# Dense experts of a gated four-layer block: the first product from half-precision parts that the pool engine makes of the weights

## The chip, the cores and the metric

One core of one Trainium2 chip runs the whole block as one program. The metric is the device time of one execution in microseconds (us), the slowest core's, and there is only one core here. Lower is better.

## The reference, cut to what matters

The block has four layers, each a gated cross-attention and a gated feed-forward part, on x of 16 batches x 112 rows x 256 columns. The change touches only the feed-forward part of layer 2: eight dense experts, expert e working on the two batches 2e and 2e+1 (224 rows).

```python
x = x + tanh(g_ffn[2]) * _L2_ffn_ref(_layernorm(x), w1, b1, w2, b2)

def _L2_ffn_ref(x, w1, b1, w2, b2):    # w1: 8 x 256 x 1024, w2: 8 x 1024 x 256
    tokens = x.reshape(E, T, D)        # E = 8 experts, T = 224 rows, D = 256
    h = jnp.einsum('etd,edf->etf', tokens, w1) + b1[:, None, :]
    h = jax.nn.gelu(h)
    y = jnp.einsum('etf,efd->etd', h, w2) + b2[:, None, :]
    return y.reshape(B, S, D)
```

## The kernel before

The program is a row of stages, each a block in which every engine has its own list of instructions; engines meet only through semaphores. A stage ends when its slowest engine ends. The dense experts are `experts_dense` (L1863), the sixth stage. Before it stands the attention of layer 2, behind it the one-head attention of layer 3 and its fp4 feed-forward part, whose weights are rounded ahead of time inside `experts_dense`.

**The body of one expert.** Every engine runs `body(turn)` through `skewed` (L1375), with `turn.i` the expert number. `there(i + 1, E)` says that a part for the next expert exists. A few turns are written out, the rest run in a loop of two turns. The order within each engine is fixed by the code.

- PE (L1997 on), in body(i): the four transposes of expert i+1's normed rows into PSUM bank 0 (L2005), which wait for the rows (`s_xn`); the second product of expert i (L2021), 2 row halves x 8 chunks with the gelu output as weights and w2 moving, which waits for the load of w2 and for all eight gelu chunks of the expert; then the first product of expert i+1 (L2031), 8 chunks f x 2 halves c of the contraction, all in float32, w1 as weights and the turned rows (224 columns) moving, into three PSUM banks in turn, each chunk waiting for the gelu of three chunks before. For the last expert eight matmuls of the next stage's weights (L2012) stand ahead of its second product.
- ACT (L1911 on), in body(i): copies expert i+1's turned rows from PSUM to `xnT` (L1921), then makes the eight gelu chunks `hT` (L1929).
- DVE (L1935 on), in body(i): norms the two batches of expert i+2 (L341, called at L1964) as soon as the transposes of i+1 have read the old ones; `gate_up_weights(i)` (called at L1968): eight steps of fp4 rounding (L2384 to L2422) on an eighth of the raw gate and up weights, 512 columns; then for each of the two batches the bias row (L1979), the residual with expert i's second product (L1983) and the statistics of the row (`row_stats`, L262 to L266, with a one-element memset of `carry`, L92, before some); then `down_weights(i)`: the same eight steps on 176 columns. The first `gate_up_weights` waits for the load of the raw fp4 weights (`s_wn`). Expert 6 adds a reciprocal root of 13 small steps (`row_rstd`), expert 7 the first rows of the next stage.
- SP issues all loads. At the start of the stage: the biases and the three raw fp4 weights (L2047, L2049, 704 KB each). In body(i): w1 of expert i+2 (1024 KB, L1856) once all first products of expert i are done (`s_h`), then w2 of expert i+1 (L1859) once the second product of expert i-1 is done (`s_y`). w1 of experts 0 and 1 and w2 of expert 0 are loaded during the attention before. All these loads go through one hardware queue.
- POOL has no block in this stage. In other stages it makes the half-precision parts of float32 tiles: a cast to float16 (L723, L784, L803) and the difference of the tile and its cast (L725, L786, L805); and it builds masks (L822), for 16 or 32 partitions, four instructions in a row.

**Where a product is already made of half-precision parts** (top-2 experts L1773, attention L1190 and L1282), each float32 operand is held as a high part (cast to float16) and a low part (rest), and three float16 matmuls stand for one in float32: high x high, high x low, low x high.

The two buffers of w1 are halves of one float32 tile (`g.fw[0]`), those of w2 halves of another (`g.fw[1]`). The lines that matter most:

```python
pe.wait_ge(s_gelu, (i + 1) * FT)                        # before the second product
held(sp, g, s_h, (i + 1) * FT)                          # before the load of w1 of expert i + 2
normed(dve, g, g.by_batch, (i + 2) * 2 + r, r).then_inc(s_xn, 1)
gate_up_weights(i)
```

## Time and profile before

| what | us |
|---|---|
| median of 3 runs | 1403.06 (1402.62 to 1405.44) |
| the profiled execution, its own time | 1411.71 |
| span of its profile, first to last instruction | 1409.9 |
| dense experts, first instruction of the block to the start of the next stage | about 1062.3 to 1179.7 |
| PE busy | 1312.7 (93% of the span) |
| DVE busy | 1105.6 (78%) |
| ACT busy | 694.4 (49%) |
| POOL busy | 414.9 (29%) |
| mean granted TensorE clock | 0.969 of 2.4 GHz |

Times in the profile count from the span's start. A float32 matmul shows as two records on PE and on PEld (the weight load), so the 16 float32 matmuls of one expert's first product are 32 records. PE's durations overlap, since matmuls are pipelined: what a series costs is read from its first start to the next thing's start. In the rows, "[1.29 <-X]" behind an instruction is the time that its engine stood idle before it, and X what ended that wait.

### The profile page before, as it was taken

What the parts mean: (1) busy time and instruction counts of PE and PEld (TensorE: products, weight loads), DVE (VectorE), ACT (ScalarE), POOL (GpSimd) and SP (SyncE); (2) the same over time, 40 slices, a digit from 0 to 9 for tenths busy, and PEclk for the clock granted to TensorE, in tenths of its full rate; (3) what the DMA queues carried; (4) which work ended last, traced back from release to release, by engine and by line L of the source; (5) the groups of instructions that cost most, each with busy time, mean ns of one, the idle gap of its engine ahead of it and who ended that gap; (6) DMA issues with size and microseconds to landing.
All of it is one profiled execution on the core that took longest, in us unless ns stands there. A gap on an engine that the chain in (4) does not pass through costs nothing. (4 is left out here: it accounts for less than half of the span.)

```text
span 1409.9 us, 36465 instructions
## 1 busy us (share of the span) xinstructions
PE 1312.7 (93%) x11864; PEld 977.7 (69%) x11864; DVE 1105.6 (78%) x3711; ACT 694.4 (49%) x1639; POOL 414.9 (29%) x580
## 2 busy tenths in 40 slices
PE   5999999899899999999899889999988998998998
PEld 3777878645457777776545568878877887885666
DVE  7788778678779988889678777676764885668997
ACT  2666767544345555555434356766753323442321
POOL 1333346434433444447134423432420000000000
PEclk8999999989989999999899999999999998999999
DMA  5544455231233333334011233333346351550000
GB/s 159 157 122 125 125 151 156 83 113 49 83 100 98 85 85 95 91 85 136 14 55 49 77 106 107 87 94 103 87 131 195 133 171 43 148 144 22 16 15 23
DMA packets 134073, 138.11 MB, mean 98 GB/s; under 512 B 38601, under 2 KB 121292, under 8 KB 133836
## 3 DMA queue, kind: packets, MB, share of 16 engines
q1 hardware_dynamic: 133948, 136.51, 33.6%
q8 instruction: 70, 1.15, 0.4%
q14 instruction: 55, 0.45, 0.1%
HBM read 100.98 MB, written 35.48 MB: 97 GB/s over the span
## 5 line engine op out<-in xcount | busy, mean ns | idle before, releaser
L1143 DVE TENSOR_REDUCE negm<-ps 112x1 f32<-112x375 f32 x512 | 260.7, 542 | 105.1 <-PE ps L1267 102.6
L1267 PE MATMUL ps<-kst,qst 96*112 96x375 f16 x768 | 232.5, 337 | 14.4 <-DVE negm L1143 7.1
L853 ACT ACTIVATE p<-ps 125x448 f32<-125x448 f32 x336 | 177.3, 543 | 110.2 <-PE ps L1295 71.9
L1282 PE MATMUL ps<-qst,kst 112*125 112x224 f16 (+1 forms) x1152 | 210.4, 265 | 8.0 <-POOL qst L822 4.3
L822 POOL TENSOR_TENSOR qst<-m_row,diag 16x448 f16<-16x448 f16 x128 | 130.3, 1046 | 280.1 <-ACT m_row L932 275.1
L1282 PEld LDWEIGHTS ps<-qst,kst 112*125 112x125 f16 (+1 forms) x1152 | 147.0, 138 | 43.1 <-issue 9.7
L1773 PE MATMUL ps<-fw,xs_e 128*128 128x512 f16 x672 | 162.7, 386 | 0.0
L1127 DVE TENSOR_SCALAR ps<-ps 125x448 f32<-125x448 f32 x192 | 120.0, 629 | 31.2 <-PE ps L1282 31.1
L1139 DVE CUSTOM_DVE_ANT_0 with_mask<-ps,mask_add 112x375 f16<-112x375 f32 x256 | 134.3, 545 | 11.5 <-issue 10.1
L1267 PEld LDWEIGHTS ps<-kst,qst 96*112 96x112 f16 x768 | 96.9, 131 | 47.5 <-DVE negm L1143 21.2
L1190 PE MATMUL ps<-wkv_split,ctxT 128*125 128x256 f16 x864 | 121.0, 277 | 0.4 <-DVE ks L1098 0.4
L1190 PE MATMUL ps<-ctxT,wkv_split 128*128 128x375 f16 (+1 forms) x552 | 107.5, 333 | 9.3 <-DVE ctxT L963 8.7
L1773 PEld LDWEIGHTS ps<-fw,xs_e 128*128 128x128 f16 x672 | 66.8, 99 | 66.7 <-issue 4.9
L822 POOL TENSOR_TENSOR mst<-m_row,mask_diag 32x448 f16<-32x448 f16 x64 | 64.1, 1031 | 158.2 <-ACT m_row L932 139.3
L1190 PEld LDWEIGHTS ps<-wkv_split,ctxT 128*125 128x125 f16 (+1 forms) x864 | 98.5, 138 | 3.0 <-issue 1.9
L853 ACT ACTIVATE p_a<-ps 125x448 f32<-125x448 f32 x144 | 78.2, 544 | 29.1 <-PE ps L1295 19.0
L1306 PE MATMUL ps<-p,v 125*32 125x112 f32 x2688 | 89.3, 266 | 0.0
L1295 PE MATMUL ps<-mst,mask_add 128*125 128x448 f16 x192 | 72.2, 385 | 12.0 <-DVE ps L1127 10.0
L1190 PEld LDWEIGHTS ps<-ctxT,wkv_split 128*128 128x128 f16 x552 | 54.3, 100 | 41.2 <-issue 14.7
L1306 PEld LDWEIGHTS ps<-p,v 125*32 125x32 f32 x2688 | 61.8, 111 | 20.1 <-issue 13.0
L2606 PE MATMUL ps<-wgu,xqT 128*128 128x512 f32 (+3 forms) x224 | 72.4, 478 | 3.4 <-DVE xh L2534 2.0
L1544 ACT ACTIVATE p<-ps,weight_e 128x256 f32<-128x256 f32 x112 | 47.0, 464 | 56.0 <-DVE weight_e L1753 52.0
(262 smaller groups left out, 2512.3 us busy)
## 6 DMA issues: line engine op xcount, KB each, us to landing
k_split<-ks SPq DMA_DIRECT2D x48, 375.0 KB, 3.6
kst<-k_split SPq DMA_DIRECT2D x96, 187.5 KB, 2.9
fw<-in_w SPq DMA_DIRECT2D x16, 1024.0 KB, 7.2
qst<-q_split SPq DMA_DIRECT2D x96, 112.0 KB, 2.4
kst<-k_split SPq DMA_DIRECT2D x96, 93.8 KB, 2.6
stage<-in_ctxT SPq DMA_DIRECT2D x16, 375.0 KB, 4.0
ctxn<-in_ctx SPq DMA_DIRECT2D x16, 375.0 KB
rows<-x SPq DMA_DIRECT2D x48, 112.9 KB, 2.8
```

The source lines that it names most:

```text
L822: pool.tensor_tensor(m_stack[q][m_rows, 4 * hg:4 * hg + 4, :], g.m_row[q][m_rows, :].rearrange("p (o s) -> p o s", o=1) .to_broadcast([n_m ...
L853: act.activation(p[p_of[hg]][kt], ps[0:KR, BK_ST + n % 2, 0:4 * S], ACT.Exp).then_inc(s_exp, 1)
L1127: dve.tensor_scalar(st, st, -CLIP, CLIP, ALU.max, ALU.min).then_inc(s_clip, 1)
L1139: dve.tensor_tensor_reduce(g.with_mask[h % 2][:, :], scored, g.mask_add[1 - par][0:S, :], 1.0, -3e38, ALU.add, ALU.max, g.maxima[1 - par][ ...
L1143: dve.tensor_reduce(g.negm[1 - par][:, h:h + 1], scored, AX_X, ALU.max, negate=True).then_inc(s_max, 1)
L1190: mm = pe.matmul(out, lhs(l, c), rhs(r, c), start=(k == 0), stop=(k == 3 * KC - 1))
L1267: mm = pe.matmul(ps[0:S, BK_S + h % 2, 0:SK], g.q_stack[q][0:96, h, :], g.k_stack[q][0:96, h // 2, :], start=True, stop=True)
L1282: mm = pe.matmul(bank[:, 2 * r * S:2 * (r + 1) * S], g.k_stack[par][0:rows, pr, kt * KR:(kt + 1) * KR], g.q_stack[par][0:rows, 2 * pr:2 * ...
L1295: pe.matmul(bank, g.mask_add[par][:, kt * KR:(kt + 1) * KR], g.m_stack[par][:, 4 * hg:4 * hg + 4, :], start=False, stop=True, skip_group_c ...
L1306: mm = pe.matmul(pv[32 * j:32 * j + 32, hg * S:(hg + 1) * S], g.v[par][:, kt, 4 * hg + j, :], p[p_of[hg]][kt][:, j * S:(j + 1) * S], start ...
L1773: mm = pe.matmul(out, lhs(l, c), rhs(r, c), start=(k == 0), stop=(k == 3 * KC - 1))
L2606: mm = pe.matmul(gate_up[w][:, first:last], xqT[:, c, :], wgu[:, w, c, first:last], start=(c == 0), stop=(c == KC - 1))
```

## The change

Expert 0 stays as it was, with its own tile `xnT0`. For experts 1 to 7 the first product becomes three float16 matmuls per chunk and half (48 of 224 columns instead of 16 in float32). POOL makes the parts of w1 in a new block (two casts of 128 x 1024 and two differences of the same size per expert, with a one-element `carry` before each cast), two experts deep. ACT's copy of the turned rows now writes their high part, and DVE makes the low part, behind the norming of the next rows and ahead of `gate_up_weights`. The load of w1 for expert i+2 no longer waits for the first product of expert i but for POOL's last difference of that expert. The second product's wait for all eight gelu chunks becomes one wait per chunk, in its first row half.

```diff
@@ -1870,6 +1870,7 @@
     s_w1, s_w2 = g.s_w1, g.s_w2
     s_xn, s_t, s_xnT, s_h, s_gelu, s_y, s_x = (sem(n) for n in ("xn", "transposed", "xnT", "h", "gelu", "y", "x"))
     s_rows, s_dve, s_m = sem("rows_counted"), sem("dve"), sem("wq_wk")
+    s_xhi, s_xlo, s_w1hi, s_w1lo, s_pool = (sem(n) for n in ("xnT_high", "xnT_low", "w1_high", "w1_low", "pool"))
     gate = g.gates[0:S, 6:7]
     FT = F // 128
     W = 2 * S
@@ -1880,7 +1881,10 @@
             return local.enter_context(nc.sbuf_tensor(f"{name}_d", shape, dt))
         b1 = sb("b1", [128, E, FT])
         b2 = sb("b2", [S, E, D])
-        xnT = [sb(f"xnT{i}", [128, KC, W]) for i in range(2)]
+        xnT0 = sb("xnT0", [128, KC, W])
+        xs = [sb(f"xs{i}", [128, 2, KC, W], F16) for i in range(2)]
+        w1s = [sb(f"w1s{i}", [128, 2, KC, F], F16) for i in range(2)]
+        turned = ps[:, 0, 0:KC * W].rearrange("p (c s) -> p c s", c=KC)
         hT = [sb(f"hT{i}", [128, FT, W]) for i in range(2)]
         acc = [sb(f"acc{i}", [S, D]) for i in range(2)]
         w1 = [g.fw[0][:, p * 2048:(p + 1) * 2048].rearrange("p (c f) -> p c f", c=KC) for p in range(2)]
@@ -1898,7 +1902,10 @@
                     i = turn.i
                     if there(i + 2, E):
 
-                        held(sp, g, s_h, (i + 1) * FT)
+                        if isinstance(i, int) and i == 0:
+                            held(sp, g, s_h, FT)
+                        else:
+                            held(sp, g, s_w1lo, i * KC)
                         load_dense(sp, a, g, Turn(turn.t + 1, turn.u), 0, s_w1)
                     if there(i + 1, E):
 
@@ -1908,6 +1915,25 @@
                         load_one_head_weights(sp, a, g)
 
                 skewed(Steps(sp, s_b), 0, 0, E - 1, 2, body)
+
+            @block.gpsimd
+            def _(pool):
+                def body(turn):
+                    i = turn.i
+                    q = 1 - turn.u
+                    if there(i + 1, E):
+                        pool.wait_ge(s_w1[q], 16 * (turn.half(1) + 1))
+
+                        if not (isinstance(i, int) and i < 2):
+                            pool.wait_ge(s_h, i * FT)
+                        for c in range(KC):
+                            carry(pool, g, c)
+                            pool.tensor_copy(w1s[q][:, 0, c, :], w1[q][:, c, :]).then_inc(s_w1hi, 1)
+                        for c in range(KC):
+                            pool.wait_ge(s_w1hi, i * KC + c + 1)
+                            pool.tensor_tensor(w1s[q][:, 1, c, :], w1[q][:, c, :], w1s[q][:, 0, c, :],
+                                               ALU.subtract).then_inc(s_w1lo, 1)
+                skewed(Steps(pool, s_pool), 0, 0, E - 2, 2, body)
 
             @block.scalar
             def _(act):
@@ -1918,8 +1944,10 @@
                     q = 1 - par
                     if there(i + 1, E):
                         act.wait_ge(s_t, i + 2)
-                        act.activation(xnT[q][:, :, :], ps[:, 0, 0:KC * W].rearrange("p (c s) -> p c s", c=KC),
-                                       ACT.Copy).then_inc(s_xnT, 1)
+                        if isinstance(i, int) and i == -1:
+                            act.activation(xnT0[:, :, :], turned, ACT.Copy).then_inc(s_xnT, 1)
+                        else:
+                            act.activation(xs[q][:, 0, :, :], turned, ACT.Copy).then_inc(s_xhi, 1)
                         for f in range(FT):
                             act.wait_ge(s_h, (i + 1) * FT + f + 1)
                             if f == 0:
@@ -1962,6 +1990,10 @@
                         at_least(dve, s_t, i + 2)
                         for r in range(2):
                             normed(dve, g, g.by_batch, (i + 2) * 2 + r, r).then_inc(s_xn, 1)
+                    if there(i, E) and there(i + 1, E):
+                        dve.wait_ge(s_xhi, i + 1)
+                        dve.tensor_tensor(xs[1 - turn.u][:, 1, :, :], turned, xs[1 - turn.u][:, 0, :, :],
+                                          ALU.subtract).then_inc(s_xlo, 1)
                     if there(i, E):
                         if isinstance(i, int) and i == 0:
                             dve.wait_ge(g.s_wn, 16 * 3)
@@ -1999,7 +2031,9 @@
                     q = 1 - par
                     if there(i + 1, E):
                         pe.wait_ge(s_xn, (i + 2) * 2)
-                        at_least(pe, s_xnT, i + 1)
+                        if isinstance(i, int) and i == 0:
+                            pe.wait_ge(s_xnT, 1)
+                        at_least(pe, s_xlo, i)
                         for r in range(2):
                             for c in range(KC):
                                 mm = pe.transpose(ps[:, 0, c * W + r * S:c * W + (r + 1) * S],
@@ -2014,22 +2048,38 @@
                         mm.then_inc(s_m, 1)
                     if there(i, E):
                         pe.wait_ge(s_w2[par], 16 * (turn.half(0) + 1))
-                        pe.wait_ge(s_gelu, (i + 1) * FT)
                         for r in range(2):
                             at_least(pe, s_x, i * 2 + r - 1)
                             for f in range(FT):
+                                if r == 0:
+                                    pe.wait_ge(s_gelu, i * FT + f + 1)
                                 mm = pe.matmul(ps[0:S, 4 + r, 0:D], hT[par][:, f, r * S:(r + 1) * S],
                                                w2[par][:, f, :], start=(f == 0), stop=(f == FT - 1))
                             mm.then_inc(s_y, 1)
                     if there(i + 1, E):
-                        pe.wait_ge(s_w1[q], 16 * (turn.half(1) + 1))
-                        pe.wait_ge(s_xnT, i + 2)
+                        whole = isinstance(i, int) and i == -1
+                        if whole:
+                            pe.wait_ge(s_w1[q], 16)
+                            pe.wait_ge(s_xnT, 1)
+                        else:
+                            pe.wait_ge(s_xlo, i + 1)
+                            pe.wait_ge(s_w1lo, (i + 1) * KC)
                         for f in range(FT):
+                            cols = slice(f * 128, (f + 1) * 128)
+                            hidden = ps[:, 1 + f % HB, 0:W]
 
                             at_least(pe, s_gelu, (i + 1) * FT + f - HB + 1)
-                            for c in range(KC):
-                                mm = pe.matmul(ps[:, 1 + f % HB, 0:W], w1[q][:, c, f * 128:(f + 1) * 128],
-                                               xnT[q][:, c, :], start=(c == 0), stop=(c == KC - 1))
+                            if whole:
+                                for c in range(KC):
+                                    mm = pe.matmul(hidden, w1[q][:, c, cols], xnT0[:, c, :], start=(c == 0),
+                                                   stop=(c == KC - 1))
+                            else:
+                                k = 0
+                                for c in range(KC):
+                                    for l, r in ((0, 0), (0, 1), (1, 0)):
+                                        mm = pe.matmul(hidden, w1s[q][:, l, c, cols], xs[q][:, r, c, :],
+                                                       start=(k == 0), stop=(k == 3 * KC - 1))
+                                        k += 1
                             mm.then_inc(s_h, 1)
                 skewed(Steps(pe, s_b), 0, -1, E - 1, 3, body)
 
```

## Rows read from the trace of the kernel before

**Rows 1.** Busy time by engine over the whole span, from the page.
```profile
PE 1312.7 (93%) x11864; PEld 977.7 (69%) x11864; DVE 1105.6 (78%) x3711; ACT 694.4 (49%) x1639; POOL 414.9 (29%) x580
```

**Rows 2.** Windows: from:to, length; busy PE, PEld, DVE, ACT, POOL; clock, DMA share, GB/s.
```profile
1105.00:1120.00 15.00, 14.67 (x74) 13.00 (x73) 13.15 (x40) 4.01 (x9) 0.00 (x0) 1.00 0.49 173
```

**Rows 3.** Timeline of PE, one expert: start, us, engine, line, operation, count, [idle before].
```profile
1094.13 6.22 PE L2031 MATMUL ps<-xnT_d,fw 128*128 128x224 f32 x32
1100.18 0.55 PE L2005 MATMUL ps<-ident,xn 112*128 112x112 f32 x4
1101.05 7.16 PE L2021 MATMUL ps<-fw,hT_d 128*112 128x256 f32 x32 [0.32 <-ACT hT_d L1929]
1108.04 6.22 PE L2031 MATMUL ps<-xnT_d,fw 128*128 128x224 f32 x32
```

**Rows 4.** Timeline of DVE, where its turns begin, and its last instruction of the stage.
```profile
1073.12 0.73 DVE L341 TENSOR_SCALAR xn<-x,rstd 112x256 f32<-112x256 f32 x2 [6.69 <-PE ps L2005]
1080.62 0.68 DVE L2384 TENSOR_REDUCE amax<-wgu_raw 88x32 f32<-88x512 f32 x1 [6.77 <-issue]
...
1091.47 0.73 DVE L341 TENSOR_SCALAR xn<-x,rstd 112x256 f32 x2
...
1103.55 0.73 DVE L341 TENSOR_SCALAR xn<-x,rstd 112x256 f32 x2
...
1178.68 0.48 DVE L1983 SCALAR_TENSOR_TENSOR x<-ps,gates,acc_d 112x256 f32<-112x256 f32 x1 [1.68 <-PE ps L2021]
```

**Rows 5.** Waits of DVE from 1080.62 to 1179.2: total us, times, longest.
```profile
DVE xn L341 <- PE ps L2005: 2.7, 2, 1.7
DVE x L1983 <- PE ps L2021: 2.2, 2, 1.7
```

**Rows 6.** Groups of POOL: busy us, mean ns of one, idle before.
```profile
L725 POOL TENSOR_TENSOR fw<-fw 128x1024 f16<-128x1024 f32 x8 | 17.0, 2130 | 0.6
L94 POOL TENSOR_TENSOR scratch<-scratch 1x1 f32<-1x1 f32 x76 | 14.2, 187 | 54.2 <-ACT qf L907 27.0 <-ACT qf L904 20.0 <-ACT stage L887 4.9
L723 POOL CAST fw<-fw 128x1024 f16<-128x1024 f32 x8 | 8.3, 1037 | 0.3
```

**Rows 7.** Timeline of an attention stretch: four POOL instructions in a row, and DVE beside them.
```profile
84.13 4.03 POOL L822 TENSOR_TENSOR qst<-m_row,diag 16x448 f16<-16x448 f16 x4 [9.24 <-ACT m_row L932]
84.21 0.99 DVE L306 TENSOR_TENSOR newton<-newton 112x5 f32<-112x5 f32 x1
85.24 0.18 DVE L264 BATCH_NORM_AGGREGATE aggregate<-stats 112x2 f32<-112x6 f32 x1
85.45 0.74 DVE L309 SCALAR_TENSOR_TENSOR rstd<-newton 112x5 f32<-112x5 f32 x1
86.23 0.96 DVE L266 COPY x<-aggregate 112x2 f32<-112x2 f32 x1
```

**Rows 8.** Groups of DVE: the low part of turned rows elsewhere, and the rounding steps.
```profile
L1098 DVE SCALAR_TENSOR_TENSOR ks<-ps,ks 128x375 f16<-128x375 f32 x32 | 17.0, 537 | 1.3 <-ACT ks L893 1.3
L1727 DVE TENSOR_TENSOR xs_e<-ps,xs_e 128x256 f16<-128x256 f32 x28 | 11.7, 418 | 5.5 <-ACT xs_e L1589 5.1
L2399 DVE SCALAR_TENSOR_TENSOR scaled<-wgu_raw,amax 88x512 f32<-88x512 f32 x8 | 5.5, 686 | 0.3
```

**Rows 9.** Timeline of PE: float16 matmuls of 224 columns, and of 256, in a row.
```profile
1054.68 0.55 PE L1282 MATMUL ps<-qst,kst 112*125 112x224 f16 x4
20.73 1.50 PE L1190 MATMUL ps<-wkv_split,ctxT 128*125 128x256 f16 x12 [0.36 <-DVE ks L1098]
```

**Rows 10.** DMA of the loads of w1(2) and w2(1), issued at 1072.8 and 1073.2.
```profile
DMA to landing us min/median/max: 10.3/11.5/12.7
```

**Rows 11.** PE around the next stage's start: timeline, then a window (columns as in rows 2).
```profile
1179.86 0.41 PE L2319 MATMUL ps<-ident,xn 112*128 112x112 f32 x2 [1.29 <-DVE scratch_dve L335]
1181.44 0.77 PE L2349 MATMUL ps<-xnT,wq_wk 128*128 128x112 f32 x2 [1.17 <-ACT xnT L2179]
...
1180.00:1190.00 10.00, 7.98 (x39) 7.02 (x39) 4.49 (x22) 3.50 (x7) 0.00 (x0) 0.56 0.25 75
```

## The prediction, made before the changed kernel was run

> **What bounds the kernel now.** I read the page's busy times first, then the windows of this stage, then the timelines of PE and DVE, DVE's waits, and last the rows of other stages that show the operations which the change adds. PE is busy 93% of the span, DVE 78% and POOL 29% [rows 1]. In the dense experts PE is busy 14.67 of 15 us at the full clock, DVE 13.15, ACT 4.01, POOL nothing [rows 2], and DMA moves at half of its share. So the stage looks like PE's, and one expert costs PE 1108.04 - 1094.13 = 13.9 us: first product 6.1, transposes 0.5 (they run into each other), an idle 0.3 until the last gelu chunk is there, second product near 7 [rows 3].
>
> The timeline of DVE tells what stands close behind. Its turns begin at 1091.47 and 1103.55: 12.1 us of its own work per expert, with no wait in them. It starts late: the first rounding waits until 1080.62 for the raw fp4 weights [rows 4]. From there to its last instruction at 1178.68 + 0.48 = 1179.16, which ends the stage, are 98.5 us, and in them it waited for PE for only 2.7 + 2.2 = 4.9 us [rows 4, 5]. Without any wait DVE would end the stage at about 1174.3. So 4.9 us is all that a faster PE can give here, whatever it saves itself.
>
> **PE's part.** The float32 product goes and 48 float16 matmuls of 224 columns come. Four such in a row take 0.55 us, the last one's own 0.26 us taken off: 0.097 each; with 256 columns twelve take 1.50, so 0.112 each [rows 9]. 48 x 0.097 = 4.7 us against 6.1: 1.4 us less for each of seven experts. The wait per gelu chunk gives back the 0.3 us of eight experts [rows 3]: the first seven chunks are made while the product runs, the eighth while the transposes and the first matmuls do. ACT is busy 4.01 of 15 us [rows 2], under 0.5 us a chunk, and a chunk now comes every 0.59 us instead of every 0.76, so it keeps up. Together PE has 9.8 + 2.4 = 12.2 us less to do, and 12.1 us per expert instead of 13.9.
>
> **DVE's part.** It gets seven differences of 448 columns from PSUM. 256 columns take 0.418 us and 375 take 0.537 [rows 8], so 1 ns a column and 0.61 for one. The first runs in the wait for the fp4 weights, between 1073.85 and 1080.62, and costs nothing; six cost 0.6 each, 3.6 us. DVE's turn is now 12.7 us, longer than PE's 12.1. Behind the waiting instruction stand the rounding and the residuals, and PE's first product waits for it; ACT's high part comes 0.5 us after the transposes, while DVE norms the next rows, so that wait is nil when DVE is late. By this alone the stage ends at 1179.16 - 4.9 + 3.6, that is 1.3 us earlier.
>
> **POOL's part.** Casts of 128 x 1024 take 1.04 us, differences 2.13, the small carries 0.19 [rows 6]: 2 x (1.04 + 2.13 + 0.19) = 6.7 us, about 7 with gaps, for each of seven experts. As a rate that fits into 12.7 us and would be free. What it does to DVE isn't. Beside four POOL instructions of 1.01 us in a row, a DVE product of two SBUF tiles of five columns takes 0.99 us instead of 0.17 and ends at 85.20, the next of the kind ends at 86.19, a copy at 87.19: each some 0.05 us after a boundary of POOL's (85.14, 86.15, 87.16), while the statistics in between take their usual 0.18 [rows 7]. So a DVE instruction with two inputs in SBUF, or a copy or scalar operation on SBUF alone, stands still until POOL's running instruction ends, and gets through between two of them; one that reads PSUM or one tile doesn't care. The Trainium skill (SBUF — State Buffer, its part on what VectorE and GpSimd share) says the same against this change: an exclusive lock on a pair of interfaces, held for the whole instruction, against copies and scalar operations of VectorE in a two-port mode and against those with two SBUF inputs. The trace agrees, by the 0.99 us above; by the page the sum is the one that follows, and a sum without it is a rival below.
>
> Of DVE's turn, the steps L2389, L2399 to L2422, L341, L1979 and L266 are of that kind; the reductions, reciprocals, residuals from PSUM, row statistics and the new difference aren't. When does POOL run? The parts of expert k+2 may start when the first product of k is done. With DVE behind, that product starts right at its difference and takes 4.7 us, as long as DVE's gate and up rounding (its steps of 0.69 us [rows 8] and smaller ones, 4.6 in all). So a burst meets DVE at the bias rows and residuals. Walked through: behind the first cast DVE has a residual, statistics and aggregate to do, 1.1 us, and loses 0.1; the second bias row waits out the second cast, 0.9; beside the first difference there is again 1.1 us of free work, and 1.0 is lost; beside the second there is one reduction of 0.33, and 1.7 is lost. That is 3.7 us. The bounds: at the best phase each cast is covered and each difference loses 1.0, 2.0 us; at the worst all 6.7 is lost, in the middle of the gate and up rounding, where nothing is free. I take 3.7, since both the phase in steady state and the first bursts (w1(2) lands 11.5 us after 1072.8 [rows 10], near 1084.3, when DVE too is at its bias rows) are near it. The burst of expert 1 starts with the stage and meets only the 6.7 us in which DVE is idle before 1073.12 [rows 4], so it costs nothing; without that cover it would push the transposes that end this wait. Six are left: 6 x 3.7 = 22.2 us.
>
> **SP's part.** w1 of expert 3 is issued once POOL has its parts of expert 1, before 1080, instead of after the first product of expert 1, behind the loads already queued, and later ones about when POOL has read the buffer; w2 stands behind it in the queue, but its own condition (a second product) comes later anyway. DMA is at half its share [rows 2], so nothing waits here. POOL's parts have nearly two turns until they are needed.
>
> **The sum.** -1.3 + 22.2 = +20.9 us, all of it in this stage: DVE ends at about 1200, its turn is 12.7 + 3.7 = 16.4 us, and PE idles some 4 us in each. The profiled execution took 1411.71 with a span of 1409.9; it would show a span near 1431. On the median of 1403.06 that gives 1424.0. About 0.2%, 2.8 us, is what a measurement of this kernel can tell from no change.
>
> **The rivals.**
> - PE's saving arrives. If DVE's lateness doesn't set the pace, the 12.2 us go off: 1390.9, faster. For it speaks that PE is busy 14.67 of 15 us [rows 2]. It decides where DVE's turn is under PE's 12.1, and its own 12.1 [rows 4] plus the difference is over that before POOL says anything. 0.05.
> - The lock is seen on small DVE instructions only; if the big ones pass beside POOL, the stage gains the 1.3 us and perhaps a little more: 1401.8, within 0.2%. It would take 1 in 10: nothing in the trace shows a 0.69 us rounding step beside a POOL instruction. Half of the lock, because DVE gets in between more often, lies between: 1413.8 at 2.0 us a burst. 0.10 for the first, the second is in my forecast.
> - PE becomes slow as well. Behind gaps of 1.29 and 1.17 us the granted clock fell to half and averaged 0.56 over 10 us [rows 11], the level of 1.2 GHz. PE would now idle 4 us in each turn. A stretch of 8.8 us at half costs it 4.4 us, about what it has idle, so +0.5 a turn, 3 us: inside my range. At half throughout, PE's turn would be 24.2 us against 16.4, 47 us more: 1471. It needs a PE that is idle and slow at once, and a PE that fills its turn gets its clock back; 0.04.
> - The change doesn't do what it says: if the wait per chunk changed nothing, PE still has the other 9.8 us, and DVE's sum is the same. No chance of its own.
>
> **How the numbers follow.** Forecast, DVE held up by POOL: 0.81. Lock without effect: 0.10, of which 0.09 within 0.2% and 0.01 faster. PE's saving arrives: 0.05. Half clock throughout: 0.04. Faster 0.06, same 0.09, slower 0.85. Range: the low end lies below the 1413.8 of the best phase, at 1407, for DVE slipping through more often; the worst phase in all six bursts would give 1403.06 - 1.3 + 40.2 = 1442, but no burst in the steady state has it, and I stop at 1437. That leaves out the two first rivals and the fourth, 0.19.
>
> **What would show it.** Right: the copies, bias rows and rounding steps beside POOL instructions take up to 1 or 2 us more and end just behind them; DVE's turns are 15.5 to 17.5 us apart with hardly a wait; PE's first product takes 4.7 us and waits for the low part `xs_d`; the stage ends near 1200. Wrong: rounding steps of 0.69 us beside a running POOL difference, turns of DVE near 12.7, or PE waiting for POOL's parts of w1 instead of DVE.

## The result, and the profile after

The changed kernel is slower. Its ratio to the kernel before, measured beside it on the same chip, is 1.0193 [1.0167, 1.0218]; on the 1402.84 us which the kernel before took there that is +27.1 us, about 1429.9. The runs were 1429.48, 1431.39 and 1437.17 us; one more, disturbed, took 1576.4 us at a mean granted clock of 0.81 instead of 0.96 to 0.97, and is left out. I had forecast +20.9 us, 1424.0: the direction and the range hold, the size is 6 us short. The profiled execution took 1429.48 us with a span of 1427.7.

| | before | after |
|---|---|---|
| dense experts: from the row statistics that open the stage to those that open the next | 1062.37 to 1179.78 = 117.4 us | 1057.72 to 1201.44 = 143.7 us |
| first rounding step, behind the stage's start | 18.2 us | 17.1 us |
| from there to DVE's last instruction | 98.5 us | 126.0 us |
| PE busy from 1090 to 1165, granted clock | 73.38 of 75 us, 1.00 | 61.66 of 75 us, 0.89 |

The stage grew by 26.3 us. The span grew by only 17.8, since this one execution of before ran long in other stages (1411.71 against a median of 1403.06), so from here on I compare lengths of the stage, and times by ratios.

The page's busy times of the kernel after, which answer to [rows 1]:
```profile
PE 1302.9 (91%) x11976; PEld 965.4 (68%) x11976; DVE 1144.2 (80%) x3718; ACT 694.2 (49%) x1639; POOL 461.8 (32%) x622
```
PE is busy for 9.8 us less, part of it at a lower clock, so that this is no measure of what the new product saves. DVE is busy for 38.6 us more: seven new instructions of 0.62 us are 4.3 us of that. The other 34.3 us are instructions that take longer than before, since the profile counts an instruction that stands still as busy.

Three windows of after (columns as in [rows 2]):
```profile
1105.00:1120.00 15.00, 11.78 (x62) 9.39 (x61) 14.07 (x30) 2.01 (x5) 4.09 (x2) 0.77 0.10 27
1120.00:1135.00 15.00, 11.06 (x67) 9.09 (x65) 13.46 (x32) 2.77 (x7) 6.63 (x6) 0.94 0.64 228
1150.00:1165.00 15.00, 13.52 (x84) 11.30 (x81) 13.84 (x30) 4.01 (x9) 6.51 (x6) 0.89 0.11 33
```
DVE runs 30 instructions in 14.07 us where it ran 40 in 13.15 [rows 2]. PE is down to between 11 and 13.5 us, and its granted clock, 1.00 (2.4 GHz) before, is a mix of that and the lower level of 1.2 GHz.

Timeline of PE, after, one expert and the start of the next (as [rows 3]):
```profile
1116.61 4.76 PE L2080 MATMUL ps<-xs_d,w1s_d 128*128 128x224 f16 x48
1121.21 0.55 PE L2039 MATMUL ps<-ident,xn 112*128 112x112 f32 x4
1121.60 7.07 PE L2056 MATMUL ps<-fw,hT_d 128*112 128x256 f32 x32
1132.61 6.43 PE L2080 MATMUL ps<-xs_d,w1s_d 128*128 128x224 f16 x48 [3.94 <-DVE xs_d L1995]
```
PE's side came out as forecast: 48 float16 matmuls in 4.76 us, no idle before the second product, and 3.94 us of idle for the low part `xs_d` before the next first product, which then takes 6.43 us: the granted clock was 0.73 in that stretch, and 1.00 during the product of 4.76 us.

Where DVE's turns begin, after (as [rows 4]):
```profile
1113.72 0.74 DVE L341 TENSOR_SCALAR xn<-x,rstd 112x256 f32 x2
1131.12 0.73 DVE L341 TENSOR_SCALAR xn<-x,rstd 112x256 f32 x2 [0.49 <-issue]
1148.29 0.74 DVE L341 TENSOR_SCALAR xn<-x,rstd 112x256 f32 x2
```
The turns are 17.40 and 17.17 us apart (the two around them 17.44 and 17.04), where I had 16.4.

Two of PE's waits from 1062 to 1205, after (total us, times, longest):
```profile
PE ps L2080 <- DVE xs_d L1995: 11.6, 4, 3.9
PE ps L2056 <- DVE x L2015: 9.7, 2, 6.5
```
Both are waits for DVE. None of PE's waits there is for POOL's parts of w1. DVE for its part doesn't wait for PE at all between its first rounding and its last instruction, where it had waited 4.9 us before [rows 5].

Four groups of DVE in the stage, after (busy us, mean ns, idle before):
```profile
L266 DVE COPY x<-aggregate 112x2 f32 (+1 forms) x14 | 24.3, 1736 | 1.4
L2472 DVE TENSOR_TENSOR wgu_raw<-scaled,qscale 88x512 f32<-88x512 f32 (+1 forms) x8 | 10.5, 1314 | 0.3
L2011 DVE SCALAR_TENSOR_TENSOR acc_d<-b_d,gates,x 112x256 f32<-112x256 f32 (+1 forms) x16 | 9.5, 592 | 0.1
L1995 DVE TENSOR_TENSOR xs_d<-ps,xs_d 128x448 f16<-128x448 f32 x7 | 4.3, 618 | 0.0
```
The copy of two numbers a row takes 1.74 us on average, and 24.3 us for all 14. One burst, in the timeline of all engines, shows how:
```profile
1138.91 0.48 DVE L2011 SCALAR_TENSOR_TENSOR acc_d<-b_d,gates,x 112x256 f32 x1
...
1139.39 1.03 POOL L1931 CAST w1s_d<-fw 128x1024 f16<-128x1024 f32 x1
...
1140.52 0.18 DVE L264 BATCH_NORM_AGGREGATE aggregate<-stats 112x2 f32<-112x6 f32 x1
1140.52 1.03 POOL L1931 CAST w1s_d<-fw 128x1024 f16<-128x1024 f32 x1
...
1140.84 4.92 DVE L266 COPY x<-aggregate 112x2 f32 x1
1141.52 4.21 POOL L1934 TENSOR_TENSOR w1s_d<-fw,w1s_d 128x1024 f16<-128x1024 f32 x2
1145.68 0.33 DVE L2434 TENSOR_REDUCE amax<-wd_raw 128x11 f32 x1
```
The copy starts beside the second cast and ends at 1145.76, 0.03 us behind the second difference (1141.52 + 4.21 = 1145.73). It doesn't get through at the end of the cast (1141.55), nor between the two differences. Over the six bursts that meet a busy DVE, the instructions that stood took 29.6 us over their own times: copies 3.97, 5.17, 3.79, 4.92 and 4.92 (own 0.17), bias rows 1.38 and 1.40 (own 0.48), rounding steps 1.54 and 5.70 (own 0.69). That is 4.9 us a burst instead of 3.7. (A Newton step that stood for 5.1 us in the burst of expert 1 makes it 34.7, the 34.3 us of the page.) A new difference costs DVE 0.55 us, from its start to that of the next instruction, 3.3 us for six. So the sum is 29.6 + 3.3 - 4.9 (waits gone) = 28.0, against 126.0 - 98.5 = 27.5 measured. The stage grew by 1.1 us less than that, since its first rounding step came 17.1 instead of 18.2 us behind the start.

### The profile page after: what moved, and what is told of

It is laid out like the page before. It is cut to its first block and busy times, and to the rows that moved or that the text cites. A ratio compares the mean times of both kernels' runs of the same rounds, so it can differ in the third digit from the quotient of the medians.

```text
span 1427.7 us, 36811 instructions
## 1 busy us (share of the span) xinstructions
PE 1302.9 (91%) x11976; PEld 965.4 (68%) x11976; DVE 1144.2 (80%) x3718; ACT 694.2 (49%) x1639; POOL 461.8 (32%) x622
## 5 line engine op out<-in xcount | busy, mean ns | idle before, releaser
L1267 PEld LDWEIGHTS ps<-kst,qst 96*112 96x112 f16 x768 | 96.6, 130 | 48.0 <-DVE negm L1143 21.2
L1957 ACT ACTIVATE hT_d<-ps,b_d 128x224 f32<-128x224 f32 x64 | 28.7, 448 | 94.4 <-PE ps L2080 83.7
L1306 PEld LDWEIGHTS ps<-p,v 125*32 125x32 f32 x2688 | 61.0, 110 | 19.9 <-issue 13.1
```

Source lines behind the costliest of these rows:

```text
L1267: mm = pe.matmul(ps[0:S, BK_S + h % 2, 0:SK], g.q_stack[q][0:96, h, :], g.k_stack[q][0:96, h // 2, :], start=True, stop=True)
L1306: mm = pe.matmul(pv[32 * j:32 * j + 32, hg * S:(hg + 1) * S], g.v[par][:, kt, 4 * hg + j, :], p[p_of[hg]][kt][:, j * S:(j + 1) * S], start ...
```

## The experiments

All are compared with the kernel before on their own chip. What they do to the stage, on the same two marks as above (before 117.4, after 143.7 us), and to DVE's stretch in it, from the first rounding step to DVE's last instruction (before 98.5 us):

| run | ratio to before | stage, us | DVE's stretch, us | turns of DVE, us |
|---|---|---|---|---|
| after | 1.0193 [1.0167, 1.0218] | 143.7 | 126.0 | 17.0 to 17.4 |
| e2 POOL's parts made once | 0.9991 [0.9973, 1.0009] | 114.5 | 96.6 | 12.4 to 12.9 |
| e3 POOL's bursts on the kernel before | 1.0134 [1.0105, 1.0164] | 136.5 | 118.3 | 16.5 to 17.8 |
| e4 waits per chunk alone | 0.9975 [0.9955, 0.9995] | 113.3 | 94.9 | 12.0 to 12.4 |
| e5 after with one gelu wait | 1.0180 [1.0155, 1.0204] | 147.7 | 129.5 | 17.4 to 18.1 |
| e1 wait between the differences | 1.0149 [1.0118, 1.0179] | 138.5 | 120.9 | 15.7 to 16.9 |
| e8 waits between all four | 1.0146 [1.0120, 1.0173] | 138.5 | 120.6 | 15.5 to 17.0 |
| e6 eight halves, all with waits | 1.0144 [1.0117, 1.0172] | 138.3 | 119.6 | 16.4 to 18.0 |
| e7 as e3, on 16 partitions | 1.0089 [1.0063, 1.0115] | 128.3 | 111.1 | 15.0 to 15.3 |
| e11 high part of w1 by ACT | 0.9981 [0.9964, 0.9997] | 115.0 | 96.6 | 12.4 to 12.9 |
| e10 as e11, norming by ACT too | 0.9936 [0.9912, 0.9961] | 110.5 | 93.2 | 11.8 to 12.0 |

The stage and the stretch are each of one execution. Where the first rounding begins isn't steady: in these executions it is between 16.6 and 18.2 us behind the stage's start, and the stage's length takes that in. DVE's stretch doesn't, so that is the one to compare where a microsecond matters.

### Is it POOL? (e2, e3)

e2: after, with POOL's parts made for expert 1 alone. It leaves out the own w1 of experts 2 to 7 from the first product, which multiplies with the parts of expert 1 in their place. The loads of w1 wait for the first products again, as in before.
```diff
-                skewed(Steps(pool, s_pool), 0, 0, E - 2, 2, body)
+                body(Turn(0, 0))
...
-                                        mm = pe.matmul(hidden, w1s[q][:, l, c, cols], xs[q][:, r, c, :],
+                                        mm = pe.matmul(hidden, w1s[1][:, l, c, cols], xs[q][:, r, c, :],
```


> The changed kernel, but POOL makes the parts of w1 for expert 1 only, and experts 2 to 7 use those (their own w1 is loaded but left out of the product); loads of w1 wait for the first product as before the change. PE, ACT and DVE do exactly what they do in the changed kernel. Theory A (POOL's bursts hold DVE up): six bursts are gone, and what is left is DVE's own 12.7 us a turn: 1.3 us under the kernel before, near 1401.5, between 1399 and 1403. Rival B (the new order costs it: the low part behind the norming, PE's gaps and its lower clock): most of the 27 us stay, above 1415. Rival C (PE is the bound as soon as POOL is quiet): near 1391.

The time is that of before, as I had expected (theory A), and far from both rivals. Where DVE's turns begin, in e2:
```profile
1101.56 0.73 DVE L341 TENSOR_SCALAR xn<-x,rstd 112x256 f32 x2
1114.49 0.73 DVE L341 TENSOR_SCALAR xn<-x,rstd 112x256 f32 x2 [0.49 <-issue]
1126.98 0.74 DVE L341 TENSOR_SCALAR xn<-x,rstd 112x256 f32 x2
```
Its window from 1090 to 1165, PE alone (length, busy, clock, DMA share, GB/s):
```profile
1090.00:1165.00 75.00, 73.59 (x508) 1.00 0.42 140
```
So the float16 product, the differences on DVE and the waits per chunk together gain 2.9 us of stage, and six bursts of POOL cost 143.7 - 114.5 = 29.2 us. PE's clock is at 1.00 again as soon as DVE no longer makes it idle, so the lower clock in after goes with the waits. It costs nothing of its own there, since DVE, which ends the stage, never waits for PE from its first rounding on.

e3 is the other half: the kernel before, and POOL makes the same four instructions in each turn from a constant tile, for nobody.
```diff
+                        for c in range(KC):
+                            carry(pool, g, c)
+                            pool.tensor_copy(w1s[:, 0, c, :], raw[:, c, :]).then_inc(s_w1hi, 1)
+                        for c in range(KC):
+                            pool.wait_ge(s_w1hi, i * KC + c + 1)
+                            pool.tensor_tensor(w1s[:, 1, c, :], raw[:, c, :], w1s[:, 0, c, :],
+                                               ALU.subtract).then_inc(s_w1lo, 1)
```


> The kernel before, with POOL's bursts added and nothing else: per expert two carries, two casts and two differences of 128 x 1024, of a constant tile into a tile that nobody reads, started by the same counts of first products as in the changed kernel. Theory A: DVE loses 4.9 us in each of six bursts and had 4.9 us of waits to give: +24 us, with 15 to 30 as the bounds since the bursts meet other parts of DVE's turn; the same copies, bias rows and rounding steps are held up. Rival B: bursts cost nothing, since they fit beside the stage, and the time stays at 1403.

It costs 19.1 us of stage, though the loads are those of before and PE and ACT do what they did: POOL's work alone is enough. I had expected 24, from six bursts, but one of the six, from 1068.4 to 1074.7, lies ahead of DVE's first rounding, where DVE has nothing to do. In the other five DVE's instructions stood 25.1 us over their own times, 5.0 a burst, and DVE's stretch agrees: 118.3 less the 93.6 that it would be without bursts and without waits (98.5 - 4.9) is 24.7. One burst of e3, in the timeline:
```profile
1114.63 5.63 DVE L2006 SCALAR_TENSOR_TENSOR acc_d<-b_d,gates,x 112x256 f32 x1
...
1114.79 1.03 POOL L1931 CAST w1s_d<-raw_d 128x1024 f16<-128x1024 f32 x1
1115.79 4.19 POOL L1934 TENSOR_TENSOR w1s_d<-raw_d,w1s_d 128x1024 f16<-128x1024 f32 x2
```
A bias row of 0.48 us stands for 5.15 us more: here too a cast and two differences hold DVE as one, whether it is at a copy, a bias row or a rounding step.

### The waits per chunk (e4, e5)

e4: the kernel before, with the change's second half alone.
```diff
-                        pe.wait_ge(s_gelu, (i + 1) * FT)
...
+                                if r == 0:
+                                    pe.wait_ge(s_gelu, i * FT + f + 1)
```


> The kernel before with the one wait for eight gelu chunks made one per chunk, and nothing else. PE saves about 0.3 us in each of eight experts, 2.4 us. Theory: DVE waited only 4.9 us for PE in all, most of it late in the stage, and gets these 2.4 us through to the end nearly whole, since the last residual waits for PE: 1 to 2.4 us faster, 1400.5 to 1402. Rival: DVE's work takes the place of the wait: no difference, within 0.5 us.

Timeline of PE, e4:
```profile
1091.38 6.22 PE L2032 MATMUL ps<-xnT_d,fw 128*128 128x224 f32 x32
1097.43 0.55 PE L2005 MATMUL ps<-ident,xn 112*128 112x112 f32 x4
1097.82 7.07 PE L2022 MATMUL ps<-fw,hT_d 128*112 128x256 f32 x32
1104.73 6.22 PE L2032 MATMUL ps<-xnT_d,fw 128*128 128x224 f32 x32
```
The idle 0.32 us of [rows 3] is gone, and more with it: from the transposes to the second product it is 0.39 us instead of 0.87, and PE's turn is 1104.73 - 1091.38 = 13.35 us instead of 13.9, 0.6 less where I had put 0.3. DVE's waits for PE fell from 4.9 us to 1.3, and its stretch by 3.7; the first rounding, 0.4 us sooner, makes the 4.1 us of stage, more than the 1 to 2.4 that I had expected. In the time it is 0.25% less [0.05, 0.45], which is 0.7 to 6.3 us.

e5: after, with the one wait for all gelu chunks put back (e4's edit reversed).

> The changed kernel with the single wait for all eight gelu chunks put back, the rest as changed. DVE sets the pace of the changed kernel and PE idles about 4 us a turn, so the 0.3 us a turn are hidden: no difference from the changed kernel, within 1 us of its stage of 143.7. Rival: PE is on the path (its lower clock), and the stage grows by 2 us or more.

The times don't tell it from after (1.0180 beside 1.0193), as I had expected. The profile has a stage 4 us longer, for which I had given 1. One burst in it is unlike those of after; timeline, e5:
```profile
1079.26 1.03 POOL L1931 CAST w1s_d<-fw 128x1024 f16<-128x1024 f32 x1
1079.30 12.10 DVE L2471 TENSOR_TENSOR wgu_raw<-scaled,qscale 88x512 f32<-88x512 f32 x1
...
1086.67 4.18 POOL L1934 TENSOR_TENSOR w1s_d<-fw,w1s_d 128x1024 f16<-128x1024 f32 x2
...
1092.37 10.09 PE L2055 MATMUL ps<-fw,hT_d 128*112 128x256 f32 x32 [11.83 <-DVE x L2015]
```
The bursts of experts 2 and 3 came back to back there, and one rounding step stood through the rest of both, 12.1 us; PE idled 11.83 us behind it and then took 10.09 us for a second product of 7.1, at a granted clock of 0.70. The rival, PE on the path, isn't it: in e5 too DVE never waits for PE from its first rounding on, and its stretch is 3.5 us longer because its instructions stood that much longer (33.1 us over their own times, 29.6 in after). In after the bursts of experts 2 and 3 follow as closely: the second difference ends at 1084.78, and POOL's next small carry starts at 1084.74. There the rounding step got in between the two, in e5 it didn't. Whether putting back the single wait has a part in that or it is chance from one execution to the next, I didn't settle.

### What holds DVE from one POOL instruction to the next (e1, e8, e6, e7)

e1: after, with a wait of POOL for its own first difference ahead of the second.
```diff
+                            if c:
+                                pool.wait_ge(s_w1lo, i * KC + c)
```


> The changed kernel, with one wait more on POOL: the second difference waits until the first is complete. In the changed kernel's profile the two differences stand as one block of 4.2 us and a copy of DVE waits out both (3.8 to 4.9 us). Theory A: two POOL instructions over 128 partitions that follow without a wait leave no gap in which DVE gets the port; a gap lets it in. Then a burst costs DVE about the 3.7 us of the prediction instead of the 4.9 measured, six bursts 7 us less: near 1423, and no copy of DVE above 2.3 us. Rival: DVE only gets in when POOL has nothing queued at all, or POOL's wait is too short for it: the copies stay near 4 us and the time near 1430.

One burst of e1, in the timeline:
```profile
1122.09 1.03 POOL L1931 CAST w1s_d<-fw 128x1024 f16<-128x1024 f32 x1
1122.13 3.10 DVE L266 COPY x<-aggregate 112x2 f32 x1
1123.09 4.52 POOL L1936 TENSOR_TENSOR w1s_d<-fw,w1s_d 128x1024 f16<-128x1024 f32 x2
...
1127.05 0.58 DVE L266 COPY x<-aggregate 112x2 f32 x1
```
The wait lets DVE in: the copy ends at 1125.23, behind the first difference, and the row's other work gets done before the second copy. That takes 5.2 us off the stage. DVE's stretch is 24.3 us over that of e2, so a burst still costs about 4.0, not the 3.7 of theory A. And the copy still spans cast and difference (3.10; I had said at most 2.3); the code shows why: the wait ahead of the first difference is for the first cast, which is done long before.

e8: waits between all four, so also between the casts and before the first difference.
```diff
+                            if c:
+                                pool.wait_ge(s_w1hi, i * 2 + c)
...
+                            if c:
+                                pool.wait_ge(s_w1lo, i * 2 + c)
+                            else:
+                                pool.wait_ge(s_w1hi, (i + 1) * 2)
```


> The changed kernel with a wait for the one before ahead of each of POOL's four large instructions (second cast, both differences). The run with one wait ahead of the second difference showed a copy of 3.1 us that still stood through the second cast and the first difference, and lost 3.3 us a burst. Theory A: each adjacency without a wait counts as one hold; with all of them gone no DVE instruction stands longer than one difference, 2.3 us beyond its own time, but the holds now meet other instructions, and what counts is how much of a burst's 6.4 us DVE spends on work that doesn't touch the port: 3 to 4 us lost a burst, a stage of 135 to 140 us, a time about that of the one gap. Rival: holds stay fused, copies of 3 to 5 us.

One burst of e8, in the timeline:
```profile
1122.69 1.03 POOL L1934 CAST w1s_d<-fw 128x1024 f16<-128x1024 f32 x1
1122.89 0.85 DVE L266 COPY x<-aggregate 112x2 f32 x1
...
1123.80 4.33 POOL L1941 TENSOR_TENSOR w1s_d<-fw,w1s_d 128x1024 f16<-128x1024 f32 x2
1124.03 1.93 DVE L2446 TENSOR_SCALAR qscale<-amax 128x11 f32<-128x11 f32 x1
...
1126.24 2.08 DVE L2456 SCALAR_TENSOR_TENSOR scaled<-wd_raw,amax 128x176 f32<-128x176 f32 x1
```
Now each DVE instruction stands until the POOL instruction beside it ends, and no longer (0.85, 1.93, 2.08): the picture that my prediction had drawn. The stage is 138.5 us, as in e1, since more is held up in smaller pieces. (The 3.3 us a burst which the expectation above gives for e1 holds for two of its bursts; over the six it is 4.0.)

e6: the same with eight pieces of 512 columns. Its core:
```diff
+                            pool.tensor_copy(w1s[q][:, 0, k, cols], w1[q][:, k, cols]).then_inc(s_w1hi, 1)
...
+                            pool.tensor_tensor(w1s[q][:, 1, k, cols], w1[q][:, k, cols], w1s[q][:, 0, k, cols],
```


> The changed kernel with POOL's four instructions cut into eight of 128 x 512 (casts near 0.57 us, differences near 1.1 us), each waiting for the one before. Theory: DVE waits out at most one short piece at each of its port instructions and does its other work meanwhile, so a burst costs it less than POOL's 6.6 us by more: 2.5 to 3.5 us, a stage of 131 to 137. Rival: the pieces meet more of DVE's port instructions, one for each, and the loss is that of whole instructions or more: 138 or above.

One burst of e6, in the timeline:
```profile
1122.58 4.86 POOL L1941 TENSOR_TENSOR w1s_d<-fw,w1s_d 128x512 f16<-128x512 f32 x4
...
1124.06 1.11 DVE L2456 SCALAR_TENSOR_TENSOR scaled<-wd_raw,amax 128x176 f32<-128x176 f32 x1
1125.20 1.11 DVE L2462 TENSOR_SCALAR magic<-scaled 128x176 int32<-128x176 int32 x1
1126.35 1.29 DVE L2468 SCALAR_TENSOR_TENSOR scaled<-magic,scaled 128x176 f32<-128x176 f32 x1
```
My theory of 131 to 137 us missed, and the rival had it: no gain. DVE steps of 0.25 and 0.34 us now take 1.1 to 1.3 us, about as long as a piece of POOL's, 1.16 us. Cut smaller, more steps are held and each for less. DVE gets one instruction in per POOL instruction, and the four differences still take 4.86 us.

e7: e3 with POOL's instructions on 16 partitions. That hardly changes POOL's durations (cast 1.07 us on average instead of 1.03, difference 2.16 instead of 2.12), only how many partitions it works on.
```diff
-                            pool.tensor_copy(w1s[:, 0, c, :], raw[:, c, :]).then_inc(s_w1hi, 1)
+                            pool.tensor_copy(w1s[96:112, 0, c, :], raw[96:112, c, :]).then_inc(s_w1hi, 1)
```


> The kernel before with POOL's bursts added, as in the earlier run of that kind, but every cast and difference on 16 partitions (96 to 111) instead of 128: the same count, order and number of columns. Before the change four POOL instructions on 16 partitions in a row let one DVE instruction through at each boundary; the changed kernel's instructions on 128 partitions without a wait between them didn't. Theory A: it is the number of partitions, so here DVE gets in between the two differences: no DVE instruction above 2.4 us, and a burst costs less, the stage 3 us or more under the 136.5 us of the run with 128 partitions. Rival B: it is the missing wait between the two differences, whatever the partitions: instructions of 4 to 5.6 us again and a stage near 136.5. Rival C: on 16 partitions there is no hold-up at all: a stage near 117.

One burst of e7, in the timeline:
```profile
1110.56 1.04 POOL L1931 CAST w1s_d<-raw_d 16x1024 f16<-16x1024 f32 x1
1110.80 0.83 DVE L266 COPY x<-aggregate 112x2 f32 x1
1111.53 2.43 DVE L2006 SCALAR_TENSOR_TENSOR acc_d<-b_d,gates,x 112x256 f32 x1
1111.56 4.39 POOL L1934 TENSOR_TENSOR w1s_d<-raw_d,w1s_d 16x1024 f16<-16x1024 f32 x2
```
With no wait between them, DVE gets through at the end of the cast and between the differences, and the longest that an instruction stands is 2.44 us in all. The stage is 128.3 instead of 136.5 us. Of these 8.2 us, 1.0 is that the first rounding came sooner (16.6 against 17.6 us behind the stage's start), and 7.2 is DVE's stretch. As in e3 five bursts met a busy DVE: 111.1 - 93.6 = 17.5 us, 3.5 a burst instead of e3's 5.0, with nothing else changed than the partitions. No run has a number between 16 and 128, or other 16 partitions than 96 to 111.

### The parts without POOL (e11, e10)

ACT is busy 4 of 15 us in this stage [rows 2]. In e11 it makes the float16 high part of w1, the product is of two parts of the rows with that one, and the waits per chunk stay. It leaves out the low part of w1, so 32 matmuls instead of 48, and nothing of POOL's work is left.
```diff
+                            act.wait_ge(s_w1[par], 16 * (turn.t + 2))
+                            for c in range(KC):
+                                act.activation(w1s[par][:, c, :], w1[par][:, c, :], ACT.Copy).then_inc(s_w1hi, 1)
```


> The same with the norming left on DVE: two float16 matmuls, high part of w1 by ACT, low part of w1 left out of the product. Theory: PE has 16 matmuls a turn less than in the run with the parts made once and DVE the same work, so if DVE sets the pace the stage is that run's, 114.5 us, within 1 us, though PE does 1.5 us a turn less. Rival: PE still has a share of the pace, and the stage is under 112.

e10 gives ACT the norming of experts 2 to 7 as well, which is 0.65 us of DVE's turn. It leaves out the same low part.
```diff
+                                act.activation(g.xn[r][0:S, :], g.x[:, b, :], ACT.Identity,
+                                               scale=g.rstd[0:S, bass.ds(b, 1)],
+                                               bias=g.shift[0:S, bass.ds(b, 1)]).then_inc(s_xn, 1)
```


> The changed kernel without POOL: ACT, which is busy 4 of 15 us, casts w1 of the next expert to float16 (two of 128 x 1024), and the product is two float16 matmuls, high part of w1 x high and low part of the rows; the low part of w1 is left out of the product. ACT also norms the rows of experts 2 to 7 in DVE's place, with one more small DVE instruction for the shift. The wait per gelu chunk stays. Theory: DVE sets the pace whenever PE is under 12 us, so what counts is DVE's turn: 12.1 + 0.6 - 0.7 = 12.0 us, PE's is near 10.6. With the 114.5 us stage of the run with the parts made once as the measure (12.7 us a turn), six turns less 0.7 give 110.3 us, between 109 and 112: 6 to 8 us under the kernel before, ratio 0.995. Rival: ACT's casts, 2 us more a turn, reach PE or DVE: a stage of 114 or more.

Two groups of ACT from 1060 to 1180, e10:
```profile
L1944 ACT ACTIVATE w1s_d<-fw 128x1024 f16<-128x1024 f32 x12 | 12.0, 1045 | 5.1 <-DMA fw<-in_w 5.1
L1938 ACT ACTIVATE xn<-x,row_shift,rstd 112x256 f32 (+1 forms) x12 | 6.5, 592 | 0.0
```
e11's stage is 115.0 us, close to that of e2: DVE's turn is the same 12.4 to 12.9 and no instruction of it stands. With the norming gone (e10) it is 11.8 to 12.0, the stage 110.5 us, and the time 0.64% under before [0.39, 0.88]. The stage was forecast at 110.3, and part of the agreement is luck: of the 4.6 us under e11, 1.1 is a first rounding that came sooner, and DVE's stretch is only 3.4 shorter, 0.6 a turn. Of all the kernels here e10 is the fastest, but it computes less. The fastest with before's own arithmetic is e4.

## Why the prediction was right, and where it was short

- **DVE bounds, not PE.** Right. PE's float16 product is shorter and PE idles for DVE instead; from its first rounding on DVE never waits for PE. e2 and e4 show what a faster PE gives here: stages of 114.5 and 113.3 us, 2.9 and 4.1 under before. The limit of 4.9 us from DVE's waits [rows 5] holds.
- **PE's product 4.7 us.** Right: 4.76 at the full clock. The wait per chunk gives PE 0.6 us a turn and not 0.3 (e4), which changes nothing in the sum, since DVE bounds.
- **DVE's new difference 0.61 us, six of them 3.6, and without POOL 1.3 us off.** Nearly: it lasts 0.618, but the next instruction starts 0.55 after it, so six cost 3.3. The turn without POOL was forecast at 12.7 and is 12.4 to 12.9 in e2. There the stage is 2.9 us shorter, not 1.3: 0.3 from this and 0.9 from a first rounding that came sooner.
- **POOL's first burst is free.** Right: it ran from 1057.8 to 1064.1 and one Newton step of DVE took 5.26 us in it, in the time in which DVE has nothing to do. The first rounding started 17.1 us behind the stage's start, no later than the 18.2 of before.
- **A burst costs 3.7 us.** This is the term that was too small: 4.9, so 29.2 us for six (143.7 - 114.5) instead of 22.2. The step that failed is that a held instruction "gets through between two of them". It came from [rows 7], where POOL's instructions are on 16 partitions. e7 shows that this is what decides it: with 16, DVE gets in, and a burst costs 3.5, about what I had taken; with 128, a cast and two differences hold it for up to 5.2 us. In my walk through the burst, 0.9 was lost to the second cast, 1.0 to the first difference and 1.7 to the second, with free work between; in reality one copy stood through all three and the free work never came beside them. Where e8 puts waits between all of them, the picture of the walk comes back, though not its price: the stage is 138.5 - 114.5 = 24.0 us over e2, 4.0 a burst. I had also put the first of the six bursts at the bias rows. It came 19.9 us behind the stage's start, not 21.9, and met the gate and up rounding, where it cost 5.9; the other five cost 4.5 to 5.0.
- **The sum.** -1.3 + 22.2 was -2.9 + 29.2 in the stage. The two errors go opposite ways, so 20.9 is nearer to the 26.3 than the price of a burst deserved. Luck, too, is that DVE ends at 1200.8 where I had said about 1200: the stage of this execution began 4.7 us earlier than that of before. And that e1, another kernel, measures the +20.9 us that I had forecast for after is no support for the walk.
- **Upper bound.** I stopped at 6.7 us for a burst and called it impossible in the steady state. For one burst that holds: the dearest of after cost 5.9. That two bursts can come back to back, as they do in after and in e5, and hold one instruction for 12.1 us, as in e5, I hadn't seen.
- **PE at a lower clock.** I had allowed 3 us for it inside the range. The granted clock did fall, to between 0.77 and 0.95 per window, and was 1.00 again from 1180 to 1195. It shows no cost of its own: DVE never waits for PE, and the account above closes to 0.5 us without it.
- **The rivals.** The lock without effect and PE's saving fall by the result, and by e2 and e3; half the clock throughout falls by the windows of after. What I had named as a sign of being right, instructions that take "up to 1 or 2 us more", wasn't seen: it was up to 5.

## What to carry to other kernels

Work on 128 partitions given to POOL "for free" cost DVE three quarters of its length here, where DVE sets the pace and many of its instructions have two inputs in SBUF or are copies or scalar operations there: 6.5 us of POOL cost 4.9 us of DVE, and neither spacing nor cutting it brought that below about 4. Look first for an engine whose work doesn't hold up the one that sets the pace (ACT's cast cost DVE nothing), and before a faster PE is paid for, add up how long the engine behind it waits for PE, since that is all it can give. When a price for such interference is taken from a trace, take it from rows with the same number of partitions.

## What the runs showed of the hardware that I had not expected

- POOL's instructions on 128 partitions, one behind the other without a wait for the one before, mostly held DVE as if they were one: 0.17 us of copy took 4.92, and a step of 0.69 took 12.10 in one run. With a wait for POOL's own last instruction between them, DVE gets one instruction in (e1, e8). On 16 partitions it gets in without one (e7, at most 2.44 us).
- The Trainium skill (SBUF — State Buffer, Who interferes with whom) has the lock held for one instruction. e8 and e7 agree, after doesn't: there it goes on into the next, and the 4.92 us of the copy decide. A sentence of the Trainium skill (GPSIMD Engine Reference, 2.1 Instruction dispatch) fits this: each of POOL's cores serves 16 partitions, and starts the next instruction as soon as its own share is done. With eight cores at work there may then be no moment in which none of them holds the lock, while with one there is. No run here shows the cores singly, so this cause is argued only.
- ACT casts 128 x 1024 from float32 to float16 in 1.045 us, about as fast as POOL (1.03), and no instruction of DVE is longer beside it (e10, e11).
- Cutting POOL's work into halves gains nothing (138.3 against 138.5 us): DVE gets in once per POOL instruction, and each of its small steps then lasts as long as a piece.
